# Setup of a fused layer kernel: other layouts for W, x, LoRA and expert weights, W2 as the loaded side

## What is computed

```
c  = x @ W + (x @ loraA[id1]) @ loraB[id1]            # "cond": per batch its own adapter, rank 16
xp = c @ x_proj_w.T                                    # 32 step-size inputs, B (16), C (16)
dt = softplus(dt_in @ dt_proj_w.T + dt_proj_b)
h_t = exp(dt * A) * h_(t-1) + dt * B * c               # scan over 64 steps, 16 states a channel
x1 = x + (C . h + D * c)
y  = x1 @ W2.T + bias2 + (x1 @ lora2A[id2].T) @ lora2B[id2].T
logits = y @ router_w.T ; gates = softmax over the two largest of 4
out = x1 + 4 * sum_e gates_e * (y @ expA[e].T) @ expB[e].T
```

## Time and profile before

| | |
|---|---|
| median of 3 runs | 938.08 us (933.51 to 939.79) |
| the profiled execution | 935.4 us, span 933.7 us |
| busy share of the span | PE 89%, PEld 81%, DVE 82%, POOL 71%, ACT 68% |
| DMA | 164,936 packets, 172.23 MB; 84,329 packets under 512 B |
| body's first product | 89.57 us after the span's start |

### The profile page before, as it was taken

The page is one execution under the profiler, slowest core; times in us unless marked ns, Lnnn a source line. Parts: engine busy times, 40 slices in busy tenths (PEclk is TensorE's granted clock), DMA queues, the critical chain, the costliest instruction groups (busy, mean ns, idle before and its releaser), DMA issues.

```text
span 933.7 us, 18414 instructions
## 1 busy us (share of the span) xinstructions
PE 828.1 (89%) x6328; PEld 757.6 (81%) x6328; DVE 762.2 (82%) x688; ACT 632.3 (68%) x1475; POOL 660.3 (71%) x343
## 2 busy tenths in 40 slices
PE   5299798889999999999998999999997999889784
PEld 4294698779988899789977998789986998678672
DVE  2234767798899989998998889988998789999993
ACT  2236667577777777767767786777777676778750
POOL 1000677568877888778877798778877787879891
PEclk9599799899999999999999999999999999989997
DMA  9984688646674758756673757575773655252321
GB/s 248 314 291 143 221 219 238 174 135 218 176 234 133 253 175 215 216 168 234 170 237 115 269 160 213 178 242 172 184 245 113 227 162 144 74 175 86 92 68 45
DMA packets 164936, 172.23 MB, mean 184 GB/s; under 512 B 84329, under 2 KB 137577, under 8 KB 156654
## 3 DMA queue, kind: packets, MB, share of 16 engines
q1 hardware_dynamic: 138796, 93.85, 36.3%
q10 hardware_dynamic: 26050, 77.21, 24.7%
HBM read 137.33 MB, written 33.69 MB: 183 GB/s over the span
## 4 chain that ended last, share of the span: by engine, by line
PE 66%; DVE 10%; ACT 6%; POOL 4%; DMA 4%; issue 4%; ACTq 2%; SPq 2%; POOLq 0%; DVEq 0%
PE jb L1030 28%; PE yp L1203 19%; PE dBx L1030 10%; DVE h L994 6%; POOL hC L564 4%; PE yp L1030 4%; PE jb L1034 3%; ACT dA L598 3%; ACTq L693 2%; PE yp L1034 2%; DMA stacked<-dtx_scratch 1%; DMA dtx_scratch<-HL 1%; PE yp L1208 1%; DMA Wst<-W_scratch 1%; DMA xin<-in_x 1%
## 5 line engine op out<-in xcount | busy, mean ns | idle before, releaser
L564 POOL TENSOR_TENSOR hC<-h,Cb 128x1024 f32<-128x1024 f32 (+1 forms) x256 | 613.9, 2400 | 174.7 <-DVE h L994 164.0
L994 DVE TENSOR_TENSOR_SCAN h<-dA,dBx 128x1024 f32<-128x1024 f32 x256 | 582.7, 2280 | 57.4 <-PE dBx L1030 47.5
L598 ACT ACTIVATE dA<-dt,negA 128x252 f32<-128x252 f32 x1024 | 430.2, 494 | 66.5 <-DVE h L994 58.0
L1203 PE MATMUL yp<-ident,hC 128*128 128x128 f32 x2048 | 280.4, 282 | 27.7 <-DVE xT L891 11.8
L1203 PEld LDWEIGHTS yp<-ident,hC 128*128 128x128 f32 x2048 | 241.5, 146 | 32.5 <-issue 26.9
L1030 PE MATMUL jb<-xT,Wst 128*128 128x256 f32 x1416 | 215.5, 295 | 0.5 <-DMA Wst<-W_scratch 0.5
L1030 PE MATMUL dBx<-Bd,stacked 96*128 96x256 f32 x1024 | 187.8, 306 | 12.1 <-DMA stacked<-dtx_scratch 6.7
L1030 PEld LDWEIGHTS jb<-xT,Wst 128*128 128x128 f32 x1416 | 183.0, 192 | 5.1 <-issue 4.1
L1030 PEld LDWEIGHTS dBx<-Bd,stacked 96*128 96x128 f32 x1024 | 145.9, 196 | 22.5 <-issue 20.3
L546 POOL TENSOR_TENSOR dtx<-dt,u 128x256 f32<-128x256 f32 x64 | 47.2, 737 | 76.2 <-DVE dt L796 75.0
L623 ACT ACTIVATE HL<-yp 128x256 fp32r<-128x256 f32 x54 | 20.4, 377 | 57.9 <-PE yp L1034 49.7
(11 more groups left out here) (165 smaller groups left out, 705.6 us busy)
## 6 DMA issues: line engine op xcount, KB each, us to landing
Wst<-W_scratch ACTq DMA_DIRECT2D x54, 1024.0 KB, 6.0
stacked<-dtx_scratch SPq DMA_DIRECT2D x192, 128.0 KB, 2.6
dtx_scratch<-HL SPq DMA_DIRECT2D x64, 256.0 KB, 3.7
Cb<-c_scratch SPq DMA_DIRECT2D x32, 512.0 KB, 5.2
xres<-in_x SPq DMA_DIRECT2D x64, 128.0 KB, 4.0
out<-obuf SPq DMA_DIRECT2D x32, 256.0 KB, 3.1
xin<-in_x ACTq DMA_DIRECT2D x26, 256.0 KB, 5.0
GB<-in_L_cond_lora_B SPq DMA_DIRECT2D x64, 64.0 KB, 5.6
```

The source lines that it names most:

```text
L564: pool.tensor_tensor(*(x[:, :, ns, :] for x in times_C(un)), ALU.mult).then_inc(hC_made, 1)
L598: act.activation(dA[:, half % NDA, :].rearrange("p (b n t) -> p b n t", b=GB_, n=HS)[:, :, n, 1:STEPS], dt[:, j % NDT, :].rearrange("p (b ...
L994: dve.tensor_tensor_scan(h[:, un % NH, :], dA[:, half % NDA, UNIT * p:UNIT * (p + 1)], dBx[un % 2][:, :], 0.0, ALU.mult, ALU.add).then_inc ...
L1203: last = pe.matmul(y, hC[:, un % NHC, P * n:P * (n + 1)], ident[:, :], is_transpose=True, start=un == 0 and n == 0, stop=False, skip_group ...
```

## The change

- W is loaded with four consecutive rows a partition, `(a p k)` instead of `(a k p)`; the runs of 256 columns stay. x is loaded in tiles of one block of 128 tokens and 512 columns, and TensorE reads it with a step of four words. LoRA A goes into `GA[p, b, k, r]` with runs of four rows (256 B), in every group. The halves of xT and GAs end up in the places where they were.
- dt_proj_w and expB are loaded with eight rows a partition, each partition one run (1 KB, and 512 B an expert), and their transposes are written to every eighth word of dtprojT and expBT (`every_eighth`). expB's loads move to SP's queue, behind LoRA A; GpSimd copies them into the old place (`expB_put`).
- The load of the bias b_raw moves to SP's queue; its split halves lie in G2 until SP moves them.
- W2's loads all stand behind `b_split` in SP's queue.
- GAs moves ahead of put_W(0) on ScalarE and ahead of W_low(2) on VectorE.
- times_W2(k) is eight products with 128 columns of W2 loaded and 68 of FT moved; the result is already G's transpose. ScalarE copies it into G2 at once; G_n and G2T fall away.
- On TensorE k = 0 to 5 of xproj move ahead of `cond` 7, times_W2(0) and (1) behind xproj, and stack(0) stands behind times_W2(2).
- The preparation of negA moves into the round of `cond` 5 on ScalarE.

```diff
-    (2, 0): [job("G2T", 0, "B"), job("cond", 1, "A", (4, 8))],
-    (2, 1): [job("stack", 4, "Y"), job("cond", 2, "A", (0, 4)), job("G2T", 1, "B")],
+    (2, 0): [job("cond", 1, "A", (4, 8))],
+    (2, 1): [job("stack", 4, "Y"), job("cond", 2, "A", (0, 4))],
...
-        xin = sb("xin", [P, 2, TT, 2 * P])
+        xin = sb("xin", [P, 2, D // 2])
...
-        GA = sb("GA", [P, K, GB_ * R])
+        GA = sb("GA", [P, GB_, K, R])
...
+        def xT_of(part, i):
+            return xT[:, part, K // 2 * (i // 2):K // 2 * (i // 2 + 1), P * (i % 2):P * (i % 2 + 1)]
...
+        expB_rows = dt[:, 0:2, :].rearrange("p j t -> p (j t)").rearrange("p (e k r) -> p e k r", e=E, k=K)
...
+        def every_eighth(rows, i):
+            return rows.rearrange("m (p k) -> m k p", k=K)[:, 4 * i:4 * i + 4, :]
...
-                eng.dma_start(Wraw[a][:, :, c], W.rearrange("(a k p) o -> a p k o", p=P, a=2)[a][:, :, c]).then_inc(s_W[quarter], 16)
+                eng.dma_start(Wraw[a][:, :, c], W.rearrange("(a p k) o -> a p k o", p=P, a=2)[a][:, :, c]).then_inc(s_W[quarter], 16)
...
-            eng.dma_start(xin_of(G, i), of_group(x_tok, G)[:, :, 2 * P * i:2 * P * (i + 1)]).then_inc(xin_in[i], 16)
+            eng.dma_start(xin_of(G, i), of_group(x_tok, G)[:, i % 2, D // 2 * (i // 2):D // 2 * (i // 2 + 1)]).then_inc(xin_in[i], 16)
...
-                                   row.rearrange("o (p k) r -> p (o k) r" if which else "o (k p) r -> p (o k) r", p=P)).then_inc(s, 16)
+                                   row.rearrange("o (p k) r -> p (o k) r", k=K) if which else
+                                   row.rearrange("o (h p k) r -> p (o h) (k r)", h=2, p=P)).then_inc(s, 16)
...
             load_lora_a(0)
+            for e in range(E):
+                sp_e.dma_start(expB_rows[:, e, :, :].rearrange("p k r -> p (k r)"), expB[e].rearrange("(p k) r -> p (k r)", k=K))\
+                    .then_inc(s_expB, 16)
             load_lora_b(0)
+            sp_e.dma_start(b_raw, dtproj_b.rearrange("(o n) -> o n", o=1)).then_inc(s_b, 16)
...
             sp_e.wait_ge(b_split, 2)
             for i in range(2):
                 sp_e.dma_start(dtprojT[3 * DTR + i:3 * DTR + i + 1, :].bitcast(fp32), b_part[i].bitcast(fp32)).then_inc(s_bias, 16)
+            for k in range(K - 1):
+                sp_e.dma_start(W2c[k], W2_rows[:, k, :]).then_inc(s_W2[k], 16)
...
+            pool.wait_ge(s_expB, 64)
+            pool.tensor_copy(expB_n.rearrange("p k (e r) -> p k e r", e=E), expB_rows.rearrange("p e k r -> p k e r")).then_inc(expB_put, 1)
...
-            for e in range(E):
-                act.dma_start(expB_n[:, :, R * e:R * (e + 1)], expB[e].rearrange("(k p) r -> p k r", p=P))\
-                    .then_inc(s_expB, 16)
             act.wait_ge(set_full, 1)
...
+            job("GAs", 0, 0, None)
             put_W(0)
             put_W(1)
             W_high(2)
-            job("GAs", 0, 0, None)
...
-                    for a in range(2):
-                        for tt in range(TT):
-                            c = (a * TT + tt) * P
-                            last = tr(psum[:, c:c + P], xin_of(g, i)[:, tt, P * a:P * (a + 1)], P)
+                    for a in range(K // 2):
+                        last = tr(psum[:, P * a:P * (a + 1)], xin_of(g, i).rearrange("t (p k) -> t k p", k=K // 2)[:, a, :], P)
...
-                for c in range(2):
-                    last = mm(yp[c][0:n, :], FT[:, k, :], W2c[k][:, 512 * c:512 * (c + 1)], k == 0, k == K - 1)
+                for t in range(K):
+                    last = mm(yp[t // 4][:, n * (t % 4):n * (t % 4 + 1)], W2c[k][:, P * t:P * (t + 1)], FT[:, k, :],
+                              k == 0 and t % 4 == 0, k == K - 1, skip_group_check=True)
...
                 if o == K - 2:
-                    times_W2(0)
-            job("xproj", 0, 0, 0, jb[0], "A", (0, 6))
+                    job("xproj", 0, 0, 0, jb[0], "A", (0, 6))
             job("xproj", 0, 0, 0, jb[0], "A", (6, K))
+            pe.wait_ge(set_taken, 3)
+            for k in range(2):
+                times_W2(k)
             pe.wait_ge(s_bias, 32)
-            times_W2(1)
             job("dtz", 0, 0, 0, jb[1], "B")
             job("dtz", 1, 0, 0, set_bank(2), None)
             job("Bst", 0, 0, 0, jb[0], "A")
-            for k in (2, 3):
+            times_W2(2)
+            job("stack", 0, 0, 0, jb[1], "B")
+            for k in (3, 4):
                 times_W2(k)
-            job("stack", 0, 0, 0, jb[1], "B")
-            times_W2(4)
```

More of the change, by code:

```diff
@@ L213, in layer_kernel @@
         b_raw = h[0:1, 0, :]
-        b_part = [expBT[0:1, :], expBT[64:65, :]]
+        b_part = [G2[64 * i:64 * i + 1, :, :].rearrange("p k m -> p (k m)")[:, 0:D].bitcast(fr) for i in range(2)]
         in_Bd = [Bd[:, NQ // 2 * i:NQ // 2 * (i + 1), :, :].rearrange("p q n t -> p (q n t)").rearrange("p (h k o) -> p h k o", h=2, k=K)
@@ L260, in layer_kernel @@
         full, taken = {}, {}
-        for _n in ["dtz", "x1T", "stack", "xT", "xr", "cond", "mid", "h2T", "gm", "out", "xproj", "Bst", "A2T", "FB", "G2T", "cF"]:
+        for _n in ["dtz", "x1T", "stack", "xT", "xr", "cond", "mid", "h2T", "gm", "out", "xproj", "Bst", "A2T", "FB", "cF"]:
             full[_n], taken[_n] = sem(_n + "_full"), sem(_n + "_taken")
-        per_group = {"dtz": K // 2, "x1T": K // 2, "stack": K, "xT": 4, "cond": K, "out": 4, "G2T": 2}
+        per_group = {"dtz": K // 2, "x1T": K // 2, "stack": K, "xT": 4, "cond": K, "out": 4}
         h2_raw, h2_masked, gated = sem("h2_raw"), sem("h2_masked"), sem("gated")
@@ L610, in job @@
                     wait(act, full["xr"], g)
-                    act.activation(GAs[:, :, 0, :], GA[:, :, :], ACT.Copy).then_inc(GAh_made, 1)
+                    act.activation(GAs[:, :, 0, :].rearrange("p k (b r) -> p k b r", b=GB_), GA[:, :, :, :].rearrange("p b k r -> p k b r"), ACT.Copy).then_inc(GAh_made, 1)
                     return
@@ L650, in job @@
                     act.activation(FB[64:P, :], psum[64:P, 0:EM + E], ACT.Copy).then_inc(taken[name], 1)
-                elif name == "G2T":
-                    act.activation(G2[:, 4 * i:4 * i + 4, 0:EM + E], psum[:, 0:4 * (EM + E)].rearrange("p (k m) -> p k m", k=4), ACT.Copy)\
-                        .then_inc(taken[name], 1)
                 elif name == "cF":
@@ L698, in _ @@
                 act.wait_ge(set_full, 2 + i)
-                c = slice(512 * i, 512 * (i + 1))
-                act.activation(dtprojT[0:DTR, c], set_bank(1 + i)[0:DTR, :], ACT.Copy).then_inc(w_hi, 1)
+                act.activation(every_eighth(dtprojT[0:DTR, :], i), set_bank(1 + i)[0:DTR, :].rearrange("m (k p) -> m k p", p=P), ACT.Copy)\
+                    .then_inc(w_hi, 1)
                 act.wait_ge(w_hi, 2 * i + 1)
-                act.activation(dtprojT[2 * DTR:3 * DTR, c], dtprojT[0:DTR, c].bitcast(fp32), ACT.Copy).then_inc(w_hi, 1)
+                act.activation(every_eighth(dtprojT[2 * DTR:3 * DTR, :], i), every_eighth(dtprojT[0:DTR, :], i).bitcast(fp32), ACT.Copy)\
+                    .then_inc(w_hi, 1)
+            job("GAs", 0, 0, None)
             put_W(0)
@@ L730, in _ @@
                         load_x(act, 1, i)
+                if o == 5:
+                    act.wait_ge(s_par, 48)
+                    act.activation(negA[:, :, :], negA[:, :, :], ACT.Exp).then_inc(s_neg, 1)
+                    act.wait_ge(s_neg, 1)
+                    act.mul(negA[:, :, :], negA[:, :, :], -1.0).then_inc(s_neg, 1)
                 if o == 3:
@@ L942, in _ @@
             for i in range(2):
-                c = slice(512 * i, 512 * (i + 1))
                 dve.wait_ge(w_hi, 2 * i + 1)
-                dve.tensor_tensor(dtprojT[DTR:2 * DTR, c], set_bank(1 + i)[0:DTR, :], dtprojT[0:DTR, c].bitcast(fp32), ALU.subtract)\
+                dve.tensor_tensor(every_eighth(dtprojT[DTR:2 * DTR, :], i), set_bank(1 + i)[0:DTR, :].rearrange("m (k p) -> m k p", p=P),
+                                  every_eighth(dtprojT[0:DTR, :], i).bitcast(fp32), ALU.subtract)\
                     .then_inc(proj_taken, 1)
+            job("GAs", 0, 0, 0, None)
             W_low(2)
-            job("GAs", 0, 0, 0, None)
             W_low(3)
@@ L1154, in job @@
                     return
-                elif name == "G2T":
-                    pe.wait_ge(gt_taken, 2)
-                    for a in range(4):
-                        last = tr(psum[:, (EM + E) * a:(EM + E) * (a + 1)], G_n[:, P * (4 * i + a):P * (4 * i + a + 1)], EM + E)
                 elif name == "cF":
```

46 lines of the change are left out of this document (16 added, 30 removed).

## The result

The changed kernel takes 929.25 us (median of 4 runs, 924.08 to 932.69) against 938.9 for the kernel before in the same session: ratio 0.989, 95% interval 0.9845 to 0.9934. A second session gave 939.25 (10 runs, 926.46 to 949.98) against 938.5, ratio 0.996 (0.990 to 1.002). Medians here are of all executions; ratios and their intervals leave out those more than 1.5% above the same kernel's fastest. The first session says about 1% less time, the second does not tell the two kernels apart, where 915 and a range of 906 to 926 were forecast. The profiled execution took 926.7 us (span 925.0), 8.7 less than that of before; packets fell from 164,936 to 131,785, those under 512 B from 84,329 to 54,633.

The account below looks back on a forecast made before the run. It took TensorE's own work as the steady bound, with the gain in the first 110 us behind an 18.2 us stall; terms summed to -22.7 from 935.4, giving 912.7, plus 2.7 for the median, hence 915 us, range 906 to 926.

Parts of the forecast that it names:

- The frame: First 110 us: one TensorE stall of 18.2 us, a slow clock behind it, then a chain of TensorE work.
- the stall's -18.2: Setup: expB's loads leave ScalarE's queue, GAs is ready before TensorE is free, and the whole wait goes, -18.2 us.
- The stepped copies: Setup copies writing every eighth word: no measured price; at twice the cost GAs is ready at 24, still level with TensorE.
- The clock: Setup from `xr` to F's transposes: without the long pause TensorE runs at the upper clock, -1.7 us beyond the stall.
- The tail of setup: From tile 6's end to the body's first product: 25.0 us in place of 22.5, so +2.5.
- W2 as the loaded side: W2's products in the new form: 1.76 to 1.97 us a k against 1.79 to 1.86, taken as 0.
- LoRA A in runs of 256 B: Group 0: LoRA A's loads issue 2.3 to 3.4 us earlier, shortening TensorE's stall and slow clock, -4 us.
- rival A: Group 0 keeps its stall because the second adapter's 64 B runs stay: -18.7, so 919 us; counted within the forecast's 0.78.
- No such stall repeats: 0: Body from 200 us on: TensorE's slices show 9 tenths throughout, so no stall like group 0's recurs, 0 us.
- B (DMA): Setup: the DMA sets the new pace and the refill waits 8 us or more, -12 to -14, 925 us; chance 0.15.
- D ("given back"): Setup, between 49 and 89 us: the earlier start meets the same waits later and loses the gain; chance 0.04.
- C: TensorE's stepped loads of x cost four times as much, +42 us, giving 957; decides from +0.18 a load; chance 0.03.

Follow-up runs that it names:

- expB_runs: Kernel before with only expB's loads changed to runs of 512 B, still in ScalarE's queue: 939.42 us, ratio 0.998.
- w2_moved: Changed kernel with the old form of W2's products (F loaded, 512 columns of W2 moved): 922.99 us, ratio 0.982.
- b2_runs: Changed kernel with four W2 products ahead of the first stack, plus the second adapter's second factor loaded in 512 B runs and copied by ScalarE: 923.63 us, ratio 0.9873.
- w_on_sp: Changed kernel with four W2 products before stack(0), group 0's second adapter later, `low` earlier, plus the body's W reads on SyncE's queue behind stacked's: 919.8 us.

## Why the prediction was wrong

*The frame* (one stall, a slow clock behind it, then a chain of TensorE work) was right, and the stall's -18.2 too: it fell whole, by the cause named, and expB_runs shows the cause alone (though not that the gain reaches the end by it alone). *The stepped copies* cost twice (1.11 to 1.24 us against 0.57 to 0.63), which was the bound taken for them; they were level, as said, with GAs ready at 23.6.

*"The clock", -1.7*: `xr` came as forecast. Tile 2 started at 30.77, not 29.5: the sum gave VectorE's mask 0.5 behind `xr` and left out that W_low(3) stands ahead of it on that engine. 1.3 short.

*"The tail of setup", +2.5*: this step failed, and it is the largest miss. Its own lengths were right: from the end of tile 6 (48.26) to stack(0) 15.7 against 15.2 forecast, the pause 1.05 against 0.9. But the pause was priced at its own length. The earlier trace rows had shown an engine that comes back slow after standing 18 us; the question whether 1 us could do the same before these products was not put. 32.0 in place of 25.0, so +9.5 and not +2.5.

*"W2 as the loaded side", 0*: at full clock 1.90 to 2.00 a k against 1.93 and 1.88 of the old form in w2_moved; right in size. What the sum had no term for is that behind the pause the clock was lost with the new form in three profiles, and kept with the old one in the only profile that has it.

*"LoRA A in runs of 256 B", -4*: the stall stayed, 4.06 against 4.10. Its four loads issue in 4.17 (before 4.94), 0.8 earlier where 2.3 to 3.4 were assumed, and the second adapter's stay at 6.58. That is rival A, whose condition the text had named; it ought to have been the forecast. The term also took the 6.36 of the landing in the earlier trace rows as given and did not ask what made it slow. The Trainium skill's rule ("DMA: Bandwidth & Descriptors", Specifications: line rate from 512 B on) pointed this way. What the runs show is the time to issue, not the rate: of the second adapter's second factor in runs of 512 B 2.80 (b2_runs), where runs of 64 B take 6.58.

*"No such stall repeats: 0"* failed as well. It was read off slices of 23 us, in which a wait of 2 to 4 us does not show. The changed kernel has 107.3 and 104.1 in groups 2 and 4; before had 105.9 in group 6. With the clean 102.8, groups 1 to 6 would be 6.3 us shorter. They take 623.1 together, against 619.0 in before: 4.1 longer by the collisions of one execution, which is luck and can go either way.

*Rivals.* B (DMA) did not come: between 24 and 48 TensorE waited for `low`, not for a refill. D ("given back") is partly true, in the body and not in the setup where it was looked for. C was false in size. The groups by shape, 190 to 880 us, before and then changed:

```profile
L1034 PEld LDWEIGHTS yp<-ident,xin 128*128 128x128 f32 x40 | 4.4, 140 | 1.4 <-DVE xT L891 1.4
```

```profile
L1035 PEld LDWEIGHTS yp<-ident,xin 128*128 128x128 f32 x40 | 5.6, 208 | 1.1 <-DVE xT L893 1.1
```

A stepped load takes 0.07 more here, under the 0.18 from which C decides, and the clean group grew by 0.2. In the setup the first eight loads of `xin` take 0.218 in both kernels, stepped or not. The Trainium skill ("SBUF — State Buffer", Door 1: The DMA port swizzle) has a penalty for each access to a new line of 16 bytes: the direction agrees in the body, and the fourfold price was the prediction's own assumption.

Summed on the profiled executions: -22.7 forecast, +7.0 for the tail, +1.3 for `low`, and 5.7 for the body and roundings make -8.7. In the body, forecast at -4.8, group 0 is 2.8 shorter behind the first product (91.0 against 93.8), groups 1 to 6 are 4.1 longer, and the rest 0.7 shorter. That group 0 is shorter with its stall unchanged has a cause that no run isolates.

## What to carry to other kernels

Ask of a pause of TensorE what it may do to the clock behind it, and do not price it at its length alone. A pause of 1 us cost 7 to 8 us here and one of 2 us elsewhere cost nothing more, so where it can be filled, fill it; an edit that changes the form of the products next to it is a place to look. A DMA costs its queue by runs: where something stands in a queue, look at what is issued ahead of it before counting its bytes. And follow what waits for that queue: in expB_runs the gain was lost in a wait for two small rows. Where two queues start transfers within a microsecond of each other and one of them is on the path, put both in one queue in the order wanted: here that took no work away and left no wait for `stacked` in groups 1 to 6 of the three profiles that have it, while in group 0 of w_on_sp the same move made W itself late. What it is worth in the median is not clear of the noise (908.93 against 913.6, in different sessions). Read the lengths of equal rounds of a loop, for slices of 23 us hide waits of 2 to 4.

## What the runs showed of the hardware

- A pause of 1.05 to 1.06 us between products with 128 columns loaded and 68 moved was followed within 2.4 us by a granted clock of 0.50 in place of 1.00, in three of three profiles. It stayed there for 17 to 27 us, with further waits of the body in the longer two. One of 1.12 us between products with 68 loaded and 512 moved was not followed by it (one profile). With ten transposes in the pause the clock stayed at 1.00 (one profile).
- Pauses of 1.5 to 2.3 us between products with 128 loaded and 256 moved left the clock at 1.00 in six profiles and were followed by 3 to 7 us at 0.50 in three.
- The same 256 KB cost a queue 16.13 us for three of four loads in runs of 64 B and 2.75 for all four in runs of 512 B. A load of 4 KB in runs of 32 B held SyncE's queue 3.0 us in one kernel, 5.9 in another and 19.3 in a third.
- Copies of ScalarE of 32x512 that write every eighth word took 1.11 to 1.24 us against 0.57 to 0.63 in place.
- Of three reads of 128 KB the last landed 2.6 us after its issue, or 6.3 to 6.4 with a 1 MB read issued on another queue just ahead of them or among them.
